# A two-layer graph network on one core: the first layer's output stage and the second layer's projections in one block, with eight key jobs computed chunk by chunk

## The reference

```python
x = x + gnn(layernorm(x), edge_index, ...)      # x is 1250 nodes x 512 features
x = x + ffn(layernorm(x))                       # a small network on nibbles
# gnn, for l in range(2):
q = ((x @ Wq[l].T + bq[l]) * scaling).reshape(n, H, DH)
k = (x @ Wk[l].T).reshape(n, H, DH)
v = (x @ Wv[l].T).reshape(n, H, DH)
# softmax over the edges of each target node, weighted sum of v -> agg
attn = agg.reshape(n, D) @ Wo[l].T + bo[l]
x = _batchnorm(x + attn, g1[l], beta1[l])       # mean and variance over the nodes
ff = jax.nn.relu(x @ W1[l].T + b1[l]) @ W2[l].T + b2[l]
x = _batchnorm(x + ff, g2[l], beta2[l])
```

## Time and profile before

| | us |
|---|---|
| median of 3 runs | 1162.79 (1160.96 to 1165.4) |
| the profiled execution | 1162.55 |
| its span, first to last instruction | 1160.8 |

### The profile page before, as it was taken

How to read it: one execution, slowest core, us unless ns; L and a number is a source line. 1 busy time by engine, 2 the same in 40 slices (tenths; PEclk the granted TensorE clock), 3 DMA queues, 4 the chain that set the end, 5 groups by cost and what they waited for, 6 DMA issues and landing times. The chain is left out here.

```text
span 1160.8 us, 19123 instructions
## 1 busy us (share of the span) xinstructions
PE 1052.4 (91%) x6706; PEld 875.8 (75%) x6706; DVE 776.3 (67%) x2429; ACT 594.1 (51%) x1108; POOL 306.8 (26%) x306
## 2 busy tenths in 40 slices
PE   4799899989899999999996799889999999989943
PEld 2577676887788888886986798778888888869831
DVE  6667566567677777774776430467777777748788
ACT  5552232447566666665333332556666666642445
POOL 1000000004444444442033000234444444312204
PEclk9899899989999999999998799989999999999986
DMA  6042311558312121142103314481121211322203
GB/s 140 23 139 87 111 30 37 120 144 198 83 36 58 37 59 36 37 125 73 38 1 130 75 47 96 109 190 36 42 54 37 58 36 37 107 83 45 51 1 89
DMA packets 51072, 85.10 MB, mean 73 GB/s; under 512 B 15518, under 2 KB 33818, under 8 KB 50724
## 3 DMA queue, kind: packets, MB, share of 16 engines
q1 hardware_dynamic: 50980, 83.92, 29.2%
HBM read 36.50 MB, written 21.61 MB: 50 GB/s over the span
## 5 line engine op out<-in xcount | busy, mean ns | idle before, releaser
L978 PE MATMUL banks<-k_stack,q_stack 128*125 128x416 f32 (+1 forms) x960 | 298.8, 398 | 10.3 <-DMA q_stack<-q_split 6.7
L1074 DVE CUSTOM_DVE_ANT_0 probs<-banks,scores_bias 125x416 f32<-125x416 f32 (+1 forms) x480 | 267.5, 583 | 59.1 <-PE banks L978 54.8
L958 POOL TENSOR_SCALAR probs<-probs,mass_inv 125x1250 f32<-125x1250 f32 x160 | 210.6, 1316 | 344.9 <-DVE mass_inv L1083 344.9
L992 PE MATMUL banks<-ident,probs 125*125 125x125 f32 x1600 | 259.9, 277 | 6.8 <-DVE probs_t L1065 4.6
L992 PEld LDWEIGHTS banks<-ident,probs 125*125 125x125 f32 x1600 | 242.4, 188 | 30.0 <-issue 22.3
L1044 ACT ACTIVATE probs<-probs,neg_peak 125x1250 f32<-125x1250 f32 x160 | 213.4, 1334 | 53.7 <-DVE neg_peak L1097 53.6
L1033 ACT ACTIVATE probs_t<-banks 125x500 f32<-125x500 f32 x320 | 152.3, 477 | 117.7 <-PE banks L992 117.7
L1007 PE MATMUL banks<-probs_t,v_pair 125*64 125x250 f32 x1600 | 186.2, 379 | 0.9 <-ACT probs_t L1033 0.9
L978 PEld LDWEIGHTS banks<-k_stack,q_stack 128*125 128x125 f32 x960 | 147.3, 191 | 38.7 <-issue 17.0
L1007 PEld LDWEIGHTS banks<-probs_t,v_pair 125*64 125x64 f32 x1600 | 107.4, 136 | 54.3 <-ACT probs_t L1033 1.3
L1065 DVE COPY probs_t<-banks 125x500 f32<-125x500 f32 x160 | 108.2, 676 | 56.4 <-PE banks L992 56.4
(11 more groups left out here) (241 smaller groups left out, 1423.3 us busy)
## 6 DMA issues: line engine op xcount, KB each, us to landing
q_stack<-q_split SPq DMA_DIRECT2D x160, 125.0 KB, 2.3
scores_bias<-edge_bias SPq DMA_DIRECT2D x8, 1171.9 KB
edge_bias<-bias_row SPq DMA_DIRECT2D x10, 585.9 KB
k_stack<-k_lo SPq DMA_DIRECT2D x16, 312.5 KB, 4.3
resid<-residual SPq DMA_DIRECT2D x2, 2500.0 KB, 10.1
values<-v_stage SPq DMA_DIRECT2D x2, 2400.0 KB
residual<-t SPq DMA_DIRECT2D x4, 625.0 KB, 2.9
xs<-in_x SPq DMA_DIRECT2D x5, 480.0 KB
```

The source lines that it names most:

```text
L958: nc.gpsimd.tensor_scalar(probs[:, u % 4, :], probs[:, u % 4, :], mass_inv[:, u % 4:u % 4 + 1], 1.0, ALU.mult, ALU.mult).then_inc(att["pro ...
L978: mm = nc.tensor.matmul(pb[0:NT, t % 5, 0:sn], q_stack[:, n % 2, half, part, tile * NT:(tile + 1) * NT], k_stack[:, head * N + s0:head * N ...
L992: mm = nc.tensor.transpose(pb[0:NT, 5 + t % 2, j * NT:(j + 1) * NT], probs[:, u % 4, (j0 + j) * NT:(j0 + j + 1) * NT], ident[0:NT, 0:NT])
L1074: nc.vector.tensor_tensor_reduce(out=probs[:, slot % 4, s0:s0 + sn], in0=pb[0:NT, t % 5, 0:sn], in1=scores_bias[:, (n % GROUPS) * GROUP + ...
```

## The change

- The block of layer 1's projections goes. Its work is appended to the output block of layer 0, on each engine behind what that engine did there. The jobs of `JOBS[1]` are renumbered so that their banks follow those of the output stage.
- The four turns of Wk become output jobs between f and g; ScalarE copies their high halves behind r_hi, VectorE subtracts the low halves behind its r_full and r_lo.
- `K_WAVE` = 8: the first eight key jobs are no longer done one after another but like f, chunk by chunk of the features, each of the eight in a bank of its own. Chunk k waits for h_lo of chunk k. The wave's jobs come right behind g. Wq's turns now follow eight key jobs, not six.
- The ring of wt_hi and wt_lo has a third place, in region RP, for Wv.
- SyncE loads wq_nat when h1_lo is complete and wv_nat when r_lo is, ahead of the residual stores. The eight loads of vec are issued after the last residual store and the last `g_done`, ahead of k_stacked. `oph` is cleared at the start of layer 1's attention.
- `scaled_bias` moves on VectorE behind the eight k_lo of the wave.
- The 70 small matmuls stay in the last layer only.

```diff
-        wt_hi = [place(f"wt_hi{r}", [P, DC, D], F32R, "RL", 16384 * (1 - r)) for r in range(2)]
-        wt_lo = [place(f"wt_lo{r}", [P, DC, D], F32R, "RL", 16384 * (1 - r) + 8192) for r in range(2)]
+        WT_AT = (("RL", 16384), ("RL", 0), ("RP", 0))
+        wt_hi = [place(f"wt_hi{r}", [P, DC, D], F32R, region, at_) for r, (region, at_) in enumerate(WT_AT)]
+        wt_lo = [place(f"wt_lo{r}", [P, DC, D], F32R, region, at_ + 8192) for r, (region, at_) in enumerate(WT_AT)]
...
-                turns("wk") + K_JOBS[0:6] + turns("wq") + K_JOBS[6:] + Q_JOBS[0:6] + turns("wv") + Q_JOBS[6:] + V_JOBS)
-        RING_OF = (dict(wq=0, wv=1, wk=0), dict(wk=0, wq=1, wv=0))
+                K_JOBS[0:8] + turns("wq") + K_JOBS[8:] + Q_JOBS[0:6] + turns("wv") + Q_JOBS[6:] + V_JOBS)
+        RING_OF = (dict(wq=0, wv=1, wk=0), dict(wk=1, wq=0, wv=2))
...
-                 tuple(t % 8 for t in range(len(JOBS[1]) + 1)))
+                 tuple((t + 2) % 8 for t in range(len(JOBS[1]) + 1)))
+        K_WAVE = 8
...
-            if layer:
-                with nc.Block(no_gpsimd_drain=True) as block:
...
+                    if layer:
+                        clear(sp, oph.values())
...
-                     + [[("f", c, n) for n in range(3) for c in range(FC)]] + [[job] for job in products("g", range(DC))])
+                     + [[("f", c, n) for n in range(3) for c in range(FC)]] + ([] if last_layer else [[("wk", i)] for i in range(DC)])
+                     + [[job] for job in products("g", range(DC))])
...
+                        sp.wait_ge(oph["h1_lo"], DC - 1)
+                        sp.wait_ge(oph["h1_lo_last"], 2)
+                        sp.dma_start(w_nat[1]["wq"][:, :, :], weight(gnn["Wq"], DC)[:, DC:2 * DC, :]).then_inc(proj["wq"], 16)
+                        for i in range(FC):
+                            sp.wait_ge(oph[f"r_lo{i}"], 3)
+                        sp.dma_start(w_nat[1]["wv"][:, :, :], weight(gnn["Wv"], DC)[:, DC:2 * DC, :]).then_inc(proj["wv"], 16)
                         for c in range(DC):
                             sp.wait_ge(oph["t_done"], DC + 1 + c + len(pieces(c)))
                             sp.dma_start(res_d[:, c, :], t2[:, c, :]).then_inc(res_stored, 16)
-                        sp.wait_ge(wk_in, 16)
+                        sp.wait_ge(oph["g_done"], 3 * DC)
+                        vectors(sp, 1)
+                        for s in q_in:
+                            sp.sem_inc(s, 1)
+                        for c in range(DC):
+                            k_stacked(sp, 1, c)
+                        sp.wait_ge(proj["copied"], len(Q_JOBS))
+                        first_bias(sp)
+                        for n in range(2):
+                            stacked(sp, n)
+                        sp.wait_ge(proj["vec"], 128)
...
-                    pe.wait_ge(oph["g_done"], len(ojobs) - 7 - g_first)
-                    keep_clock(len(ojobs) % 8, 70)
+                    if last_layer:
+                        pe.wait_ge(oph["g_done"], len(ojobs) - 7 - g_first)
+                        keep_clock(len(ojobs) % 8, 70)
+                        return
+
+                    assert BANKS[1][0] == len(ojobs) % 8
+                    r = RING_OF[1]["wk"]
+                    pe.wait_ge(oph["done"], turned_at[-1] + 1)
+                    for k in range(DC):
+                        pe.wait_ge(oph["h_lo" if k < DC - 1 else "h_lo_last"], k + 1 if k < DC - 1 else 2)
+                        for t in range(K_WAVE):
+                            if k == 0:
+                                pe.wait_ge(oph["g_done"], len(ojobs) - 8 + t + 1 - g_first)
+                            _, c, n = JOBS[1][t]
+                            s0, sn = CHUNKS[n]
+                            for s, (w, h) in enumerate(((wt_hi[r], h_hi), (wt_lo[r], h_hi), (wt_hi[r], h_lo))):
+                                mm = nc.tensor.matmul(pb[:, bank_of(1, t), 0:sn], w[:, k, c * P:(c + 1) * P], h[:, k, s0:s0 + sn],
+                                                      start=k + s == 0, stop=k == DC - 1 and s == 2)
+                            if k == DC - 1:
+                                mm.then_inc(proj["filled"], 1)
+                    for t in range(K_WAVE, len(JOBS[1])):
+                        project(pe, 1, t)
...
+                    for t in turned_at[DC + 4:]:
+                        weights(t)
...
                         high(1, DC - 1, h_hi, t2)
+                        for t in range(len(JOBS[1])):
+                            projected(act, 1, t)
...
                         low(dve, nc.vector, DC - 1, t2, h_hi, h_lo, "h_hi", "h_lo_last")
+                        for t, job in enumerate(JOBS[1]):
+                            if t == K_WAVE:
+                                scaled_bias(dve)
+                            if job[0] in SPLIT:
+                                reduced(dve, 1, t)
```

More of the change, by code:

```diff
@@ L1105, in gnn_ffn @@
                      + [[job] for job in products("o", (2, 3))]
-                     + [[("f", c, n) for n in range(3) for c in range(FC)]] + [[job] for job in products("g", range(DC))])
+                     + [[("f", c, n) for n in range(3) for c in range(FC)]] + ([] if last_layer else [[("wk", i)] for i in range(DC)])
+                     + [[job] for job in products("g", range(DC))])
             ojobs = [job for wave in waves for job in wave]
             g_first = ojobs.index(("g", 0, 0))
-            turned_at = [t for t, job in enumerate(ojobs) if job[0] in ("wo", "w1", "w2")]
+            turned_at = [t for t, job in enumerate(ojobs) if job[0] in ("wo", "w1", "w2", "wk")]
+            first_turned = turned_at[:DC + 4]
             def weight_part(kind, i):
+                if kind == "wk":
+                    r = RING_OF[1]["wk"]
+                    return wt_hi[r][:, i, :], wt_lo[r][:, i, :]
                 if kind == "w1":
@@ L1191, in _ @@
                         pool.wait_ge(oph["h_lo"], DC - 1)
+                        pool.wait_ge(proj["copied"], len(Q_JOBS))
+                        for n in range(2):
+                            split(pool, n)
                 @block.tensor
@@ L1197, in _ @@
                         kind = wave[0][0]
-                        if kind in ("wo", "w1", "w2"):
+                        if kind in ("wo", "w1", "w2", "wk"):
                             t, i, bank = first, wave[0][1], pb[:, first % 8, :]
@@ L1202, in _ @@
                             if i == 0:
-                                pe.wait_ge(oph[kind], 16)
+                                pe.wait_ge(wk_in if kind == "wk" else oph[kind], 16)
                             if kind == "w1":
@@ L1206, in _ @@
                             else:
-                                nat = wo_nat if kind == "wo" else w2_nat
+                                nat = dict(wo=wo_nat, w2=w2_nat, wk=w_nat[1]["wk"])[kind]
                                 blocks = [nat[:, c, i * P:(i + 1) * P] for c in range(DC)]
@@ L1240, in _ @@
                                     mm.then_inc(oph["filled"], 1)
-                    pe.wait_ge(oph["g_done"], len(ojobs) - 7 - g_first)
-                    keep_clock(len(ojobs) % 8, 70)
+                    if last_layer:
[3 more added lines that the diff above has]
+                    assert BANKS[1][0] == len(ojobs) % 8
+                    r = RING_OF[1]["wk"]
+                    pe.wait_ge(oph["done"], turned_at[-1] + 1)
[13 more added lines that the diff above has]
+                        project(pe, 1, t)
+                    bank_freed(pe, 1, former(1, len(JOBS[1])))
+                    keep_clock(bank_of(1, len(JOBS[1])), 12)
                 @block.scalar
@@ L1264, in _ @@
                         weights(turned_at[c])
-                    for t in turned_at[DC:]:
+                    for t in first_turned[DC:]:
                         weights(t)
```

2 lines of the change are left out of this document (1 added, 1 removed).

## The result

| | before | after |
|---|---|---|
| median, us | 1163.93 (1160.96 to 1165.4, 4 runs) | 1135.69 (1131.28 to 1137.21, 4 runs) |
| profiled execution's span, us | 1160.8 | 1135.4 |
| mean granted clock | 0.964 | 0.969 |

The ratio is 0.9756, with a 95% interval of 0.9731 to 0.9781. The change makes the kernel some 28 us faster; 26.3 were forecast (1136.5 us, range 1133.5 to 1143.5). Executions of the changed kernel differ by up to 5.9 us and the interval allows a gain of 25.5 to 31.3 us, so the agreement of the total to 0.8 us is partly luck; the trace is the finer test.

What follows compares the result with a forecast made beforehand. TensorE, busy 91%, was held at the layers' seam by the batch norm's serial tail and VectorE's wait for vec. The first query product moves 26.5 us earlier, less 0.3 for g: 1136.5 us, range 1133.5 to 1143.5.

Steps and rivals of the forecast that it cites:

- The anchor and the sum: Layer 1's first query product on TensorE moves from 676.93 to 650.45, 26.5 us; less 0.3 for g, 26.2.
- SyncE's clearing: Clearing of semaphores moved to the start of attention: taken at 0, 2.7 us if nothing covered it.
- The g stage: Wk's turns and split between f and g: 0.3 us; as rival, 2.5 to 4.1 us, chance 0.08.
- The wave: Eight key jobs, chunk by chunk behind g, follow the batch norm's tail and end at 638.0.
- Emptying the banks: After the eight key jobs, banks free too slowly for Wq's turns and the ninth job: 1.6 us lost.
- The wait for k_stacked: VectorE's seventh k_lo waits for the k_stacked DMA; hidden from TensorE, slack 0.8 us.
- The late handoff: Rival: slow vec loads (16.3 us) delay k_stacked, TensorE waits 7.0 us: 1143.5 us; chance 0.12.
- No overlap: Rival: chunks 0 to 2 held until the batch norm's tail ends, 12.1 us later: 1148.5 us; chance 0.05.
- The low clock: Rival: TensorE falls to 1.2 GHz in the bursts and stays there until the v jobs: 1180 us; chance 0.03.

Runs made afterwards that it cites:

- e8: The changed kernel with each of Wk's four turns done twice between f and g (32 transposes instead of 16): 1134.47 us, one run.
- e7: The changed kernel with the eight vec loads issued four times (32 issues), ahead of k_stacked: 1149.13 us, one run.
- e3: The changed kernel without its wave, the first eight key jobs done whole, one after another, without fillers: 1148.33 us, ratio 0.9862.
- e5: The changed kernel with a wave of six key jobs instead of eight: 1137.4 us, one run.
- e1: The kernel before with only the scaled bias moved on VectorE, behind the first six k_lo: 1148.57 us, ratio 0.9869.
- e6: The changed kernel with the scaled bias put back to the head of VectorE's projection work: 1143.88 us, one run.
- e2: The kernel before with the eight vec loads issued ahead of the loads of Wq and Wv: 1158.54 us, ratio 0.9955.
- e10: The changed kernel with the batch norm's one-column shift as a tensor_scalar instead of a scalar_tensor_tensor: 1132.91 us, one run.

## Why the prediction was right

- **The anchor and the sum.** 26.2 us were forecast for the first query product, 26.22 came. Behind it nothing moved: attention's first product still follows the block's fillers at the same distance (710.90 - 708.84 and 736.17 - 734.11, 2.06 us both), though SyncE's clearing now stands there; its price was 0.
- **The g stage**, taken at 0.3 us, cost 0.02: this term of the sum was mis-sized. VectorE's first statistics came at 605.10, in the clock of before 604.2, as forecast (604.4), and its backlog was gone before the second chunk. The 0.3 came from setting the transposes (1.67 us) against the profile's 1.4 us of waits; e8 shows a cover of 2.04. The price of 4.1 us, if GpSimd held VectorE's subtractions, did not come up either: the four took 2.47 us with GpSimd's third r_lo beside the first two, as without it (2.48).
- **The wave.** Starts of chunks 1, 2 and the end of the wave were forecast at 623.4, 628.8 and 638.0; less 0.87 they came at 623.5, 628.8 and 638.0.
- **Emptying the banks.** The ninth key job was forecast at 641.25 and came, less 0.87, at 641.46; the two waits that it stands behind are those of 0.57 us in the rows above. (They are counted from the modelled end of the product before; from start to start, against the pitch of the transposes, some 1.8 us are lost, where 1.6 were taken.) The four key jobs behind it took 9.27 us, not 9.2. These 0.3 us too little in the sum and the 0.3 us too much in the g stage cancel, which is luck: 650.75 was forecast with both, 650.73 came.
- **The wait for k_stacked** was there, 1.27 us long, and hidden. The vec loads took 4.9 us to issue where I took 8.6; since the third key job is split no earlier than 639.85, that gained nothing, as said.
- **The late handoff** did not happen. e7 brings it about on purpose, and prices it higher than the prediction: the rival had 7.0 us of wait at a full clock; e7's wait is longer, 9.10 us, and costs 2.2 us more by the clock. What 7.0 us would cost there was not measured.
- **No overlap** did not happen. e3 comes near it (three quarters of one job of eight still overlap): 10.25 us, where 12.1 were priced for none.
- **The low clock** did not come: waits of 0.42 to 0.57 us in bursts of 24 products leave 1.00, and so do the waits of 1.68 and 1.52 us between bursts of 18 in e5 (1.00 from 619 to 640). e3 shows that the fear was not idle: with 4.46 and 3.74 us of wait around groups of three products the same seam fell to the 1.2 GHz level. The psum-queue rule of the Trainium skill that the prediction weighed (TensorE: Matmul & The Clock Gate, section A second HAM failure mode: psum-queue depth-cycling) is not borne out by waits of this size here.

Of the 26.22 us of distance, taken in this order, 11.56 come from the bias leaving VectorE's head (e1), 4.41 more from the merged block with Wk turned early (e3 against e1; e3 also lacks the fillers, and no run parts the block's end, the early turns and the early loads), 10.25 from the wave. The order matters: the bias's place alone costs 1.57 in the changed kernel (e6).

## What to carry to other kernels

Look at what stands at the head of an engine's queue at a stage's start: one tiny instruction with an operand that nobody needs yet held the whole stage for 10 us, and moving it alone shortened the distance by 44% of what the whole change did. Where a reduction's tail leaves TensorE idle, work that can start on finished chunks, one accumulation to a bank, fills it and replaces filler matmuls; count how fast the banks can be emptied afterwards, since all come due at once. And find the moved work's cover before trusting it: 16 transposes cost 0.02 us where TensorE had waited, the next 16 cost 1.35, and the idle time in the profile's rows (1.4 us) understated the cover (2.04 us).

## What the hardware showed

- **Small loads behind large ones.** Eight loads of 1 to 2 KB (four elements to a partition, two for b1, and not one as said above) took SyncE 8.64 us to issue behind two loads of 1 MB, 4.24 us without them in front (e2), 4.87 us behind a residual store (the change) and 4.3, 4.3 and 5.0 us for the three further eights of e7.
- **VectorE and GpSimd.** A one-column scalar_tensor_tensor takes 0.22 us, and 1.9 to 2.5 us where GpSimd subtracts two tensors in SBUF; in another form it takes 0.27 and the next 1250-column scaling takes 2.85 instead of 0.93 (e10). Four subtractions with one input in PSUM were not held: they took 2.47 us in the changed kernel (602.71 to 605.18), the first two beside GpSimd's r_lo, and 2.48 before without it.

```profile
602.86 1.09 POOL L1096 TENSOR_TENSOR r_lo<-r_full,r_hi 128x416 fp32r<-128x416 f32 x1 [1.09 <-DVE r_full L1381]
```

The Trainium skill (SBUF — State Buffer, section Who interferes with whom) says that a VectorE instruction with two SBUF inputs contends with a GpSimd instruction that reads SBUF, that one in a two-port mode contends with GpSimd, and that one with at most one SBUF input outside these modes does not. The small instruction in both forms and the subtractions fit it; the wide scaling fits if it runs in a two-port mode, which no row shows.
